# Reordering VectorE's residual sum, a norm's bound and a read-back in a three-layer transformer kernel

## What is computed

```python
# layer A: 16 heads of 16, sliding window of 128 tokens, MLP of 1024
h = layer_norm(x, ln1_g, ln1_b); q, k, v = split(h @ w_qkv.T)
x = x + attn(q, k, v) @ w_o.T
x = x + gelu(layer_norm(x, ln2_g, ln2_b) @ mlp_w1.T + mlp_b1) @ mlp_w2.T + mlp_b2
x = _layernorm(x_in + x)
# layer B, twice: 8 heads of 64, window 128, gated MLP of 682
h = shift_token(x); q, k, v = split(h @ wqkv)
q = l2norm(q) * qs; k = l2norm(k) * ksc          # l2norm: t / clip(norm(t), 1e-12)
q, k = rotary_xpos(q, k)
x = x + local_attention(q, k, v) @ wo
h = layer_norm(shift_token(x)) @ w1 + b1; a, g = split(h)
x = x + (a * gelu(g)) @ w2 + b2
# at the end
x = _layernorm(x_in_of_B + x)
```

## Time and profile before

| | us |
|---|---|
| median of 3 runs | 1875.1 (1874.62 to 1875.91) |
| the profiled execution, time | 1873.0 |
| its span | 1871.3 |
| TensorE busy | 1707.7 (91%) |
| VectorE busy | 1556.7 (83%) |
| ScalarE busy | 1171.6 (63%) |
| GpSimd busy | 1042.7 (56%) |
| granted clock of TensorE, mean | 0.991 |
| first later attention, about | 554 to 1022 |
| second later attention, about | 1210 to 1672 |

### The profile page before, as it was taken

The page is one execution under the profiler, slowest core; times in us unless marked ns, Lnnn a source line. Parts: engine busy times, 40 slices in busy tenths (PEclk is TensorE's granted clock), DMA queues, the critical chain, the costliest instruction groups (busy, mean ns, idle before and its releaser), DMA issues.

```text
span 1871.3 us, 43289 instructions
## 1 busy us (share of the span) xinstructions
PE 1707.7 (91%) x15168; PEld 1470.2 (79%) x15168; DVE 1556.7 (83%) x3862; ACT 1171.6 (63%) x3024; POOL 1042.7 (56%) x996
## 2 busy tenths in 40 slices
PE   6999999899998888888888999988888888889997
PEld 5777777799986777777776888867777777778886
DVE  7898888778878898888886777788888889866776
ACT  6999988744456677676674343466767767643332
POOL 3676565434335666766663455566666765624443
PEclk9999999999999999999999999999999999999999
DMA  2111210032313222222213434132122222132221
GB/s 102 41 40 36 67 38 28 24 124 78 111 46 100 67 66 57 72 61 63 70 46 109 145 104 124 62 117 70 58 67 65 62 68 60 56 98 68 79 79 34
DMA packets 183075, 133.83 MB, mean 72 GB/s; under 512 B 21080, under 2 KB 182112, under 8 KB 182112
## 3 DMA queue, kind: packets, MB, share of 16 engines
q1 hardware_dynamic: 182880, 131.37, 23.0%
HBM read 92.52 MB, written 38.80 MB: 70 GB/s over the span
## 4 chain that ended last, share of the span: by engine, by line
PE 48%; ACT 20%; DVE 17%; issue 11%; DMA 2%; SPq 1%; POOL 0%; DVEq 0%; ACTq 0%; POOLq 0%
PE psum L595 11%; PE psum L597 11%; PE psum L596 11%; ACT b_probs L1855 10%; DVE masked L1355 3%; PE psum L710 3%; PE psum L899 3%; PE psum L692 3%; DVE q_t_lo L1339 2%; ACT a_probs L1736 2%; DVE g_in L1301 2%; ACT b_pt L1864 2%; DVE k_t_lo L1334 2%; ACT q_sq L1825 2%; ACT k_t_hi L1837 2%
## 5 line engine op out<-in xcount | busy, mean ns | idle before, releaser
L1855 ACT ACTIVATE b_probs<-masked,neg_max 128x256 f32<-128x256 f32 (+1 forms) x512 | 249.9, 490 | 217.2 <-DVE neg_max L1355 217.2
L595 PE MATMUL psum<-wa_hi,b_h_hi 128*128 128x512 f32 (+1 forms) x576 | 233.9, 406 | 5.2 <-DVE wa_lo L1150 3.6
L1355 DVE CUSTOM_DVE_ANT_0 masked<-psum,mask 128x256 f32<-128x256 f32 (+1 forms) x512 | 177.3, 412 | 69.4 <-PE psum L899 69.4
L596 PE MATMUL psum<-wa_lo,b_h_hi 128*128 128x512 f32 (+1 forms) x576 | 214.4, 372 | 0.0
L597 PE MATMUL psum<-wa_hi,b_h_lo 128*128 128x512 f32 (+1 forms) x576 | 213.7, 371 | 0.0
L595 PE MATMUL psum<-g_h_hi,wm_hi 128*128 128x512 f32 (+1 forms) x480 | 190.2, 396 | 1.2 <-DVE y_out L1388 1.0
L2080 POOL TENSOR_TENSOR g_in<-g_in,minus_half 128x16 f32<-128x16 f32 x64 | 187.9, 2936 | 4.5 <-DVE g_in L1307 4.5
L597 PE MATMUL psum<-g_h_hi,wm_lo 128*128 128x512 f32 (+1 forms) x480 | 189.2, 394 | 0.0
L596 PE MATMUL psum<-g_h_lo,wm_hi 128*128 128x512 f32 (+1 forms) x480 | 189.1, 394 | 0.0
L1475 POOL TENSOR_TENSOR g_in<-g_z,g_in 128x512 f32<-128x512 f32 x62 | 80.3, 1295 | 169.8 <-DVE g_in L1301 164.7
L899 PE MATMUL psum<-k_t_hi,q_t_hi 64*128 64x256 f32 (+1 forms) x512 | 84.5, 301 | 97.6 <-DVE y_out L1388 90.0
(11 more groups left out here) (167 smaller groups left out, 5576.9 us busy)
## 6 DMA issues: line engine op xcount, KB each, us to landing
b_inv_t<-inverse_rows SPq DMA_DIRECT2D x128, 128.0 KB, 3.0
x_mid<-y_out SPq DMA_DIRECT2D x96, 128.0 KB, 1.7
rope_in<-in_rope SPq DMA_DIRECT2D x64, 128.0 KB, 2.2
x_res<-x_state SPq DMA_DIRECT2D x64, 128.0 KB, 2.3
g_in<-x_mid SPq DMA_DIRECT2D x32, 256.0 KB, 3.7
g_old<-x_state SPq DMA_DIRECT2D x16, 512.0 KB, 4.0
out_x<-g_fin SPq DMA_DIRECT2D x15, 512.0 KB, 2.9
w_raw<-in_w_mlp_b SPq DMA_DIRECT2D x2, 2154.0 KB, 8.9
```

Source lines behind the costliest of these rows:

```text
L595: nc.tensor.matmul(out, a_hi, b_hi, start=first, stop=False)
L596: nc.tensor.matmul(out, a_hi, b_lo, start=False, stop=False)
L1355: ins = nc.vector.tensor_tensor_reduce(out[:, at], src[:, at], (mask if now else mask0)[:, at], -1.0, BIG, ALU.add, ALU.min, neg_max[:, r, ...
L1855: ins = nc.scalar.activation(out, src, ACT.Exp, bias=neg_max[:, r, k:k + 1], scale=-1.0, accum_out=row_sum[:, n % 2, 4 * r + k:4 * r + k + 1])
```

## The change

It has four parts.

1. A tile `least`, 128 x 16, is filled with 1e-24 at the start, and the bound of the queries' and keys' squared norms is an element-wise maximum of two tensors instead of a tensor and a constant.
2. In `dve_attention` the queries' `norms(s + 2, 0)` move behind `add_residual(s - 2)`, from chunk 3 on.
3. For chunk 2 (step 0) the queries' norms move the other way, ahead of `h_low`, `k_t_low` and `q_t_low`.
4. In `sp_attention`, step 30, the opening of the MLP's loads is cut in two. `spread_inverse(30)` now comes behind the first group's three loads and ahead of `vec_b`, `row_b2` and the second group's three loads. In attention A the two halves are issued back to back, as before.

```diff
+        least = sbuf("least", [P, 16])
...
-                    sp_mlp(sp, MLP_A, MA, None, opening=True)
+                    sp_mlp(sp, MLP_A, MA, None, opening="first")
+                    sp_mlp(sp, MLP_A, MA, None, opening="second")
...
                 if b_chunk(s):
                     store_inverse(s)
                 if s == NCH - 2:
-                    sp_mlp(sp, MLP_B, MB, layer, opening=True)
+                    sp_mlp(sp, MLP_B, MB, layer, opening="first")
                 if b_chunk(s):
                     spread_inverse(s)
+                if s == NCH - 2:
+                    sp_mlp(sp, MLP_B, MB, layer, opening="second")
...
-            if opening:
+            if opening == "first":
                 if c is MLP_B:
                     sp.wait_ge(SB["q_rot"], (layer + 1) * NCH)
                     sp.wait_ge(SB["k_rot"], (layer + 1) * NCH)
                 load(0, 0)
+                return
+            if opening == "second":
...
-                    nc.vector.tensor_scalar_max(norm2c[:], norm2[:], 1e-24).then_inc(S["norm2_ready"], 1)
+                    nc.vector.tensor_tensor(norm2c[:], norm2[:], least[:], ALU.max).then_inc(S["norm2_ready"], 1)
...
                 if b_chunk(s):
                     copy_probs(s, 1)
+                if s == 0:
+                    norms(s + 2, 0)
...
                 if b_chunk(s + 1):
                     k_t_low(s + 1)
                     q_t_low(s + 1)
-                if b_chunk(s + 2) and s + 2 > 1:
-                    norms(s + 2, 0)
                 if s == -1:
                     h_low(2)
                     dve_mlp(v, *mlp_behind(layer), None if layer == 0 else layer - 1, opening="finish_stats")
                 if b_chunk(s - 2) and s not in (NCH - 2, NCH - 1):
                     add_residual(s - 2)
+                if b_chunk(s + 2) and s + 2 > 2:
+                    norms(s + 2, 0)
...
+            nc.vector.memset(least[:], 1e-24)
```

## The result

| | before | after |
|---|---|---|
| median, us | 1875.5 (1874.6 to 1876.1, 4 runs) | 1781.1 (1780.4 to 1782.2, 4 runs) |
| the profiled execution, time | 1873.0 | 1780.4 |
| its span | 1871.3 | 1778.7 |
| granted clock, mean | 0.991 | 0.993 |

The ratio is 0.9498, 95% interval 0.9481 to 0.9514: 94 us less, where 88 were forecast (from a median before of 1875.1 us over three runs; a fourth makes it 1875.5). In the changed kernel most lines have moved down: L1355 is now L1361, L1301 L1307, L1307 L1313, L1388 L1394, L899 L905, L1381 L1387, L1330 L1336, L1475 L1483, L1509 L1517; on GpSimd L2074 is L2083, L2084 L2093, L2080 L2089, L2063 L2072, L1150 L1156; on SyncE L435 is L437 and L444 is L446.

What follows compares the result with a forecast made beforehand. Bound: a ring through VectorE's tail, whose late residual sum left TensorE's scores idle 90.0 us in 56 waits. 81.2 (chunks) + 6.8 (spread) = 88.0 us; 1875.1 - 88.0 = 1787.1 us, range 1776 to 1808, chance 0.75.

Steps and rivals of the forecast that it cites:

- rival 1: Later attentions' chunks: bound escapes GpSimd, or TensorE limits anyway; 0.1 us x 56 more saved, 1781 us; chance 0.10.
- (a): VectorE, steps 2 to 29: residual sum ahead of queries' norms ends at 10.96 instead of 12.73 us; TensorE allows minimum at 12.22.
- (b): VectorE's bound against a constants tensor: still held by GpSimd, form worth 0; chunk 12.32 instead of 13.89 us, 1.57 less.
- (c): GpSimd's moved work in chunks where it also splits weights: holds a VectorE instruction, 0.2 us lost each, bounds 0 and 0.7.
- (d): All chunks: 56 waits of 90.0 us, less 5.6 and 16 x 0.2 for weight chunks, give 81.2 us.
- (e): Step 0, chunk 2's queries' norms moved early: 0.8 to 1.75 us vanish into zero-row waits, nothing; without cover up to 3.5.
- (f): SyncE, step 30, spread of inverse sums between loads: VectorE's waits vanish and normalize shortens, 6.8 us, bounds 2 and 9.
- (g): The tile least and its memset, run once ahead of the first load's landing: costs nothing.
- Rival 2: VectorE's bound is also held by GpSimd's o_lo: 1.28 us return in each of 56 chunks, 1859 us; chance 0.04.
- Rival 3: GpSimd's power (L2080) holds VectorE's queries' rotation: loops change by -6 us, time stays about 1874 us; chance 0.04.
- Rival 4: TensorE's granted clock falls in the two attentions: gain gone at 0.88 of full speed, 1885 us at 0.86; chance 0.03.
- Rival 5: Later attentions: the reorder does nothing because something else ending with y_out holds TensorE; no size or chance given.

Runs made afterwards that it cites:

- the kernel with the addition: The changed kernel with VectorE's bound removed and GpSimd adding 1e-24 to the 16 sums ahead of its power: 1786.2 us, ratio 0.9529.

## Why the prediction was right

The forecast was 1787.1 us and the median is 1781.1, inside the range of 1776 to 1808. The mechanism is the one forecast. The time taken by itself would fit rival 1 as well, which had 1781; its chunk of 12.22 us and its bound of 0.2 us are not what the trace shows, and the 6 us come from elsewhere, as worked out below.

(a) *The residual sum ahead of the norms*: shown. The kernel with that edit alone has 83 of the 94 us. The ring, the late `y_out` and the scores behind it were the bound, and the next limiter was where the prediction had put it: TensorE at 12.22 (12.19 without a bound), VectorE's held bound at 12.32 (12.35).

(b) *The form*: shown to be worth nothing, in the old place and in the new one. Rival 1 falls with it, as the bound does not escape; what the rival would have given is known now, 0.16 us a chunk and not 0.1. The chunk is 0.03 us longer than forecast because L2083 takes 1.30 us, where the earlier trace rows had 1.26; the first maximum starts 0.05 us ahead of its end, as forecast.

(c) *The chunks with weights*: 12.42 to 12.45 (12.36 and 12.37 in chunk 17), 0.1 us over the others, where 0.2 was taken; in one of them L1336 took 1.38 us for two where a plain chunk has 1.28. It was not free by much: 0.3 us more on GpSimd made it 0.8.

(d) *All chunks*: 81.2 forecast, 80.9 in the profile. The one row of 56 waits carried the estimate, but that it fits to 0.3 us is in part luck: from chunk 2 on, where the edit works, the gain is 82.6, and chunks 0 and 1 took 1.7 back.

(e) *Step 0*: nothing forecast. Steps 0 and 1 together are 0.6 and 1.1 us longer in the profile of the changed kernel than in that of before, and vary by more between executions. Step 0 takes 1.0 us longer in both attentions; that the waits for the row of zeros take this up in step 1 is not shown.

(f) *The spread*: 6.8 forecast, 8.3 in the profile of the changed kernel, 6.9 in that of the spread alone and 8.0 by its time. In the profile of the spread alone VectorE's statistics of the MLP's norm also waited 1.27 and 0.52 us for a load of the first group, in the changed kernel's 0.31 and 0. The mechanism is as told: the spreads are issued from 951.21, behind three loads, and VectorE's `scale_o(30)` waits for nothing, and `normalize` is 1.34 instead of 2.29.

```profile
950.60 0.51 SPq L499 DMA_DIRECT2D g_in<-x_mid  x1
951.21 1.26 SPq L446 DMA_DIRECT2D b_inv_t<-inverse_rows  x2
952.51 0.60 SPq L535 DMA_DIRECT2D vec_b<-in_vec_b  x1
```

```profile
957.33 0.42 DVE L1394 TENSOR_TENSOR y_out<-psum,x_res 128x256 f32<-128x256 f32 x1
957.67 0.68 DVE L1387 TENSOR_TENSOR b_o<-psum,b_inv_t 128x512 f32<-128x512 f32 x1
958.63 1.34 DVE L1517 TENSOR_SCALAR g_z<-g_in,g_mv,g_rstd 128x256 f32<-128x256 f32 x4
```

The size was off because the sum stopped at VectorE and put TensorE's share into the bounds alone. TensorE at the end of the first later attention, before:

```profile
1007.90 1.94 PE L1036 MATMUL psum<-ident,g_z 128*128 128x128 f32 x8 [4.66 <-DVE g_z L1509]
1009.77 3.68 PE L931 MATMUL psum<-b_pt,v_tok 128*64 128x128 f32 x32
```

and after:

```profile
960.11 1.06 PE L1042 MATMUL psum<-ident,g_z 128*128 128x128 f32 x8 [1.15 <-DVE g_z L1517]
961.11 1.97 PE L937 MATMUL psum<-b_pt,v_tok 128*64 128x128 f32 x32
...
965.91 0.47 PE L601 MATMUL psum<-g_h_hi,wm_hi 128*128 128x512 f32 x1 [1.22 <-POOL g_h_lo L2129]
```

The idle time falls by 3.5 us (3.1 in the second attention, 4.06 to 1.00). The transposes and products behind it fall from 5.6 us to 3.0 (from 1.61 + 3.04 to the same 3.0 in the second): 2.6 and 1.6. And a wait of 1.22 us, in both, stands ahead of the MLP's first product, where there was none in the first and 0.20 in the second: GpSimd's `g_h_lo` is late next. 3.5 + 3.1 + 2.6 + 1.6 - 2.2 = 8.6, where 8.3 are measured. The term that was mis-sized is that of the faster resumption, 4.2 us, and the new wait behind it.

(g) *The tile*: nothing forecast, and 2.1 us in the trace, all in MLP A, whose code the change doesn't touch. The prediction looked at what the memset costs, and not at the tiles that `least` moves by 64 bytes in each partition.

What remains is 1.3 us in other stages, nearly all of it in attention A, which no part of the change explains and which is within what executions differ by. And the median before lay 2.1 us above the profiled execution, that of after 0.7. So 88.0 becomes 94.0: -0.3 in the loops, +1.5 in (f), +2.1 in (g), +1.3 elsewhere, +1.4 by the medians.

The other rivals. Rival 2 (the bound loses to `o_lo` as well) is out: it ends 0.03 us after L2083, while L2093 runs. Rival 3 (the power holds the queries' rotation) is out: L2089 runs from 880.67 to 883.58, L1483 starts at 882.19 inside it and takes 0.69 us, as ever. Rival 4 (less clock) is out: TensorE is busy for the whole of a chunk and keeps full speed. Rival 5 (the reorder does nothing) is out by the kernel with the order alone. One steady chunk, length, busy time of TensorE, its weight loads, VectorE, ScalarE, GpSimd, then the granted clock:

```profile
867.08:879.43 12.35, 12.35 (x116) 10.68 (x116) 12.12 (x35) 9.41 (x27) 8.83 (x8) 1.00 0.25 68
```

## What to carry to other kernels

Where an engine's list puts a side product ahead of the instruction that frees another engine's buffer, look at what the side product really takes: here 0.7 us of a reduce and 1 us of waiting behind GpSimd stood ahead of a 0.4 us read of a PSUM bank, and swapping them was worth 1.5 us in every chunk. The estimate is sound if the next limiter of the ring is worked out on each engine, and the row that says who waited for the instruction, in how many waits, gives its sum. Slack has to be read in the step that has least of it: 0.3 us more on GpSimd were free in the plain chunks and cost 0.6 in those with a piece of weights. And a new tile is not free of effects because its memset is: stages that the change doesn't touch are worth comparing stretch by stretch, over several kernels with and without it, since medians of 12 and 23 runs could not show 2 us here.

## What the runs showed of the hardware that was not expected

*GpSimd's power over 16 columns didn't hold VectorE, its sums over 512 did.* Of two-operand VectorE instructions beside GpSimd, those that met a sum or a difference over 512 columns were held to its end (the bound: 0.17 us alone, 0.97 held; 1.33 beside the 539 columns of a piece of weights), in either form, tensor with constant or with tensor. Those that met the power over 16 columns (L2089, 2.91 us) were not: 0.69 us. The Trainium skill (SBUF — State Buffer, Who interferes with whom) has a VectorE instruction with two SBUF inputs contend with a GpSimd instruction that reads SBUF, and makes no difference between a sum and a power. The trace agrees for the sums and disagrees for the power. Whether the operation or the width makes the difference no run tells. The other way round the power was held: in the first later attention of the kernel with the addition it took 3.23 to 3.33 us in the nine chunks in which VectorE's L1481 had started ahead of it, as in the one shown (662.25 against 662.51), and less than 2.95 in all others. So these rows fit a power that holds VectorE, if at all, only around its start, and not for its length.

*Half clock after an idle TensorE.* In the kernel before, L1036 and L931 ran slowly behind idle times of 4.66 and 4.06 us; TensorE's clock there and in the changed kernel (stretch, length, busy, granted clock, DMA share, GB/s):

```profile
1009.00:1012.00 3.00, 3.00 (x26) 0.50 0.65 194
```

```profile
958.00:962.00 4.00, 2.85 (x32) 1.00 0.51 147
```

0.50 is the lower of the two levels, 1.2 GHz, 1.00 the upper, 2.4 GHz. The kernel with the order alone, which keeps the late spread, has both the idle time and the slow products:

```profile
967.93 1.94 PE L1036 MATMUL psum<-ident,g_z 128*128 128x128 f32 x8 [3.97 <-DVE g_z L1509]
969.80 3.68 PE L931 MATMUL psum<-b_pt,v_tok 128*64 128x128 f32 x32
```

That with the spread alone has neither:

```profile
1006.91 1.07 PE L1041 MATMUL psum<-ident,g_z 128*128 128x128 f32 x8 [1.15 <-DVE g_z L1514]
1007.91 1.97 PE L936 MATMUL psum<-b_pt,v_tok 128*64 128x128 f32 x32
```

So the wait that the spread removes cost its own length and up to 2.6 us of slow products after it. All eleven profiles agree: in the four kernels with the late spread the products behind the idle times, of 3.74 to 4.66 us, ran slowly in both attentions, and in the seven others, with 0.81 to 1.16 us, in neither. That the idle time is the cause of the lower clock is what they fit; no run varied it by itself.
